# Gated cross-attention and ternary feed-forward block: two weight pieces scaled on GpSimd, one load and three steps of the start reordered

## What is computed

```python
x = x + tanh(g_xattn) * (softmax(q k^T / 8) v @ Wo + bo)      # q from layernorm(x), k and v from the context, 8 heads
g = bitlinear(layernorm(x), w_gate)                            # bitlinear: activations rounded to 8 bits per row,
u = bitlinear(layernorm(x), w_up)                              # weights to -1, 0, 1 by their mean magnitude
x = x + tanh(g_ffn) * bitlinear(square(relu(g)) * u, w_down)
```

## Time and profile before

| | before |
|---|---|
| time, median of 3 runs | 1199.75 us (1198.95 to 1201.97) |
| the profiled execution | 1198.77 us, span 1197.0 us |
| TensorE busy | 1177.8 us (98%) |
| DVE busy | 1032.1 us (86%) |
| ScalarE busy | 868.9 us (73%) |
| GpSimd busy | 306.5 us (26%) |
| longest chain | PE 88%, DVE 5%, DMA 3%, ACT 2% |

### The profile page before, as it was taken

The page is one execution under the profiler, slowest core; times in us unless marked ns, Lnnn a source line. Parts: engine busy times, 40 slices in busy tenths (PEclk is TensorE's granted clock), DMA queues, the critical chain, the costliest instruction groups (busy, mean ns, idle before and its releaser), DMA issues.

```text
span 1197.0 us, 18708 instructions
## 1 busy us (share of the span) xinstructions
PE 1177.8 (98%) x5859; PEld 743.8 (62%) x5859; DVE 1032.1 (86%) x2123; ACT 868.9 (73%) x928; POOL 306.5 (26%) x313
## 2 busy tenths in 40 slices
PE   8998999999999999999999999999999999999997
PEld 7655566656665666666566656665666666566653
DVE  4888898888989888888998888889898888888876
ACT  4877767777886777677877767776787677767763
POOL 3231222222442222222442222222244222222200
PEclk9999999999999999999999999999999999999999
DMA  9695535444444464344444464444444444344422
GB/s 353 251 294 125 148 96 102 114 101 99 96 114 98 112 176 110 95 104 106 101 99 101 114 182 102 97 113 98 107 97 106 96 98 114 101 99 100 98 65 57
DMA packets 286269, 144.61 MB, mean 121 GB/s; under 512 B 254509, under 2 KB 254893, under 8 KB 283684
## 3 DMA queue, kind: packets, MB, share of 16 engines
q1 hardware_dynamic: 286240, 144.32, 47.3%
q10 hardware_dynamic: 4, 0.00, 0.0%
HBM read 57.86 MB, written 24.35 MB: 69 GB/s over the span
## 4 chain that ended last, share of the span: by engine, by line
PE 88%; DVE 5%; DMA 3%; ACT 2%; issue 2%; SPq 0%; POOL 0%; DVEq 0%; ACTq 0%
PE gu_ps L1020 35%; PE o_ps L988 18%; PE s_ps L66 17%; PE y_ps L1034 17%; DMA v_scr<-x 1%; DMA xf_sb<-in_x_feat 1%; DVE half_max L1269 1%; PE gu_ps L1147 1%; DMA x_sb<-in_x_tok 0%; DVE staged L1376 0%; DVE staged L1263 0%; ACT staged L754 0%; ACT staged L797 0%; PE gu_ps L1119 0%; ACT staged L760 0%
## 5 line engine op out<-in xcount | busy, mean ns | idle before, releaser
L1020 PE MATMUL gu_ps<-w_gate,xq_t 128*128 128x512 bf16 x1016 | 240.9, 380 | 7.6 <-DVE staged L1263 7.6
L1020 PE MATMUL gu_ps<-w_up,xq_t 128*128 128x512 bf16 x1024 | 241.9, 379 | 0.0
L1034 PE MATMUL y_ps<-w_down,hq_t 128*128 128x512 bf16 x1008 | 228.0, 379 | 1.4 <-DMA hq_t<-staged 1.3
L988 PE MATMUL o_ps<-v_sb,pt_high 128*128 128x512 f32 (+1 forms) x640 | 212.9, 413 | 0.7 <-DVE pt_low L1252 0.7
L1263 DVE TENSOR_TENSOR staged<-staged,gu_ps 128x1024 f32<-128x1024 f32 x128 | 155.6, 1215 | 61.4 <-ACT staged L760 61.4
L66 PE MATMUL s_ps<-a_sb,xf_high 128*128 128x308 f32 x1024 | 187.3, 305 | 0.0
L1020 PEld LDWEIGHTS gu_ps<-w_up,xq_t 128*128 128x128 bf16 x1024 | 100.3, 98 | 120.8 <-ACT staged L754 0.3
L620 POOL TENSOR_TENSOR rstd<-var_eps,neg_half 128x1 f32<-128x1 f32 x128 | 95.7, 747 | 307.6 <-DVE var_eps L1228 269.5
L1034 PEld LDWEIGHTS y_ps<-w_down,hq_t 128*128 128x128 bf16 x1008 | 98.6, 98 | 120.7 <-DMA hq_t<-staged 1.8
L797 ACT ACTIVATE staged<-staged,h_scale 128x1024 f32<-128x1024 f32 x126 | 137.9, 1141 | 46.1 <-DVE h_scale L1283 46.1
L1020 PEld LDWEIGHTS gu_ps<-w_gate,xq_t 128*128 128x128 bf16 x1016 | 94.3, 98 | 120.1 <-issue 5.6
(11 more groups left out here) (142 smaller groups left out, 1439.3 us busy)
## 6 DMA issues: line engine op xcount, KB each, us to landing
xf_sb<-in_x_feat SPq DMA_DIRECT2D x64, 256.0 KB, 2.6
x_sb<-in_x_tok SPq DMA_DIRECT2D x64, 256.0 KB, 2.8
y<-staged SPq DMA_DIRECT2D x64, 256.0 KB, 2.1
staged<-in_wg_t SPq DMA_DIRECT2D x4, 1024.0 KB, 10.5
staged<-in_wd_t SPq DMA_DIRECT2D x4, 1024.0 KB, 7.2
folded<-a_scr SPq DMA_DIRECT2D x3, 1232.0 KB, 5.8
v_scr<-x SPq DMA_DIRECT2D x12, 256.0 KB, 2.8
folded<-v_scr SPq DMA_DIRECT2D x3, 1024.0 KB, 4.9
```

What stands on the lines that cost most here:

```text
L988: last = nc.tensor.matmul(o_ps[:, :], pt[0:rows, P * c:P * (c + 1)], v_sb[0:rows, v, c, :], start=(c == 0 and pt is pt_high and v == 0), s ...
L1020: last = nc.tensor.matmul(target[:, q, :], xq_t[:, s.par(0), c, :], w[:, c, cols], start=(c == 0), stop=(c == DC - 1))
L1034: last = nc.tensor.matmul(y_ps[:, :], hq_t[:, c, :], w_down[:, c, :], start=(c == 0), stop=(c == FC - 1))
```

## The change

- SP loads the value weights ahead of the query weights.
- `scale(2, 2)` and `scale(2, 3)` go from ScalarE's step 0 to GpSimd, behind `normalise(start, 2)` and ahead of its step 0, as one tensor_scalar each (multiply, add; 128 x 2048, float32).
- In step 1 ScalarE does `relu_half(1, 0)` and `square_half(1, 0)` first, ahead of `part_probs(3)` and `mark_hidden(0)`.
- On DVE `probs_low` of tile 1 goes from the head of step 0 to between `ternary(2, 0)` and `ternary(2, 1)`.

```diff
@@ SP, start
                 sp.dma_start(wkv_sb[:, 0, 2, :], wk[:, 2, :]).then_inc(wk_loaded[2], 16)
+                sp.dma_start(wkv_sb[:, 1, :, :], wv).then_inc(wv_loaded, 16)
                 sp.dma_start(wq_sb, wq_t).then_inc(q_loaded, 16)
-                sp.dma_start(wkv_sb[:, 1, :, :], wv).then_inc(wv_loaded, 16)
@@ GpSimd
+                def scale(m, p):
+
+                    pool.wait_ge(unit_inv_done, m + 1)
+                    pool.wait_ge(weight_stage[m][p], MEASURED)
+                    nc.gpsimd.tensor_scalar(scaled_slot(m, p), raw(m, p), inv_unit[:, m:m + 1], ROUND,
+                                            ALU.mult, ALU.add).then_inc(weight_stage[m][p], 1)
+
...
                 normalise(start, 2)
+                scale(2, 2)
+                scale(2, 3)
                 steps_by_batch(pool, step, (2, 3, 4, 5), split_keys, split_values)
@@ ScalarE, step
                 def step(s, split=None, b=None):
+                    if s.opens(1):
+                        relu_half(s, 0)
+                        square_half(s, 0)
                     if s.has(2):
                         part_probs(s, 2)
...
-                    if s.has(0):
+                    if s.has(0) and not s.opens(1):
                         relu_half(s, 0)
                         square_half(s, 0)
-                    if s.opens(0):
-                        scale(2, 2)
-                        scale(2, 3)
@@ VectorE, step and start
-                    if s.has(1) and not s.opens(1):
+                    if s.has(1) and not s.opens(0) and not s.opens(1):
                         probs_low(s, 1)
...
                 ternary(2, 0, w_down)
+                probs_low(start, 1)
                 ternary(2, 1, w_down)
```

## The result

The changed kernel takes 1202.4 us (median of 20 runs) against 1199.98 for the kernel before (20 runs). The ratio is 1.0023, 95% interval 1.0017 to 1.0029: 2.8 us slower, with 2.0 to 3.5 as the interval. One of its runs took 1335 us at a granted clock of 0.85 and is not part of the ratio. The forecast was +2.8 us. The loss is under the 0.3% (3.6 us) that the prediction named as what can be told from no change, but its interval leaves out 0.

A forecast was written before the change was run, and what follows sets the result against it. The prediction took DVE as the path from 84.78 us on, with TensorE's gaps its shadow. Its terms 0 - 0.3 + 0.8 - 1.0 + 3.3 = +2.8 us on 1199.75 gave 1202.6 us, range 1198.0 to 1206.5.

The forecast's parts named there:

- Part 1: Start, value weights loaded first: project_values gap goes, fold_keys(1, 0) still starts at 25.73; 0 us, bounds -1.7 and +0.5.
- Part 2: DVE, pt_low of tile 1 ahead of ternary(2, 1): TensorE's 0.75 us gap goes; -0.3 us, bounds -0.4 and 0.
- Part 3: ScalarE without two scales: GpSimd's low_part(4) comes earlier and meets DVE's centred; +0.8 us, bounds 0 and +1.0.
- Part 4: ScalarE step 1, relu and square first: hidden_half(1, 0) earlier, mark_input(2) then limits; -1.0 us, bounds -1.4 and 0.
- Part 5: Two scales on GpSimd, 1.9 us each: DVE waits for them and runs late; +3.3 us, bounds 0 and +9.7.
- my deduction of 0.26: DVE beside GpSimd's scales: each delays DVE by its 1.9 us length less 0.26, 3.3 us for two.
- A: Rival: GpSimd's scale is slow, over 2.3 us each, taking the sum past +3.6 us; chance 0.27.
- B: Rival: DVE keeps the ports, hiding the first scale; +1.2 us, 1200.9 us; chance 0.09.
- C: Rival: DVE-GpSimd exclusion costs nothing here; -0.5 us, 1199.2, or 1198.4 without the low_part(4) collision; chance 0.08.
- D: Rival: faster, the load order's 1.78 us comes through; -3.0 us, 1196.7, if exclusion also costs nothing; chance 0.06.

The follow-up runs named there:

- e1: Kernel before with only the value weights loaded ahead of the query weights; ratio 0.9998 (0.9989 to 1.0007).
- e4: Kernel before with only pt_low of tile 1 moved between the two ternary pieces on DVE; ratio 0.9992 (0.9984 to 1.0001).
- e2: Kernel before with only the two down-piece scales moved from ScalarE to GpSimd; ratio 1.0044 (1.0031 to 1.0058).
- e11: Kernel before, scales left on ScalarE, plus two GpSimd operations of the same shape on other data that nobody waits for; ratio 1.0047 (1.0033 to 1.0060).
- e5: Changed kernel with the old load order; ratio 1.0016 (1.0007 to 1.0025) against the kernel before.
- e3: Kernel before with only relu and square first in ScalarE's step 1; ratio 0.9988 (0.9977 to 0.9998).
- e7: Changed kernel with GpSimd scaling only 1024 of 2048 columns of each piece, the rest left unscaled; ratio 0.9999 (0.9990 to 1.0008) against the kernel before.
- e9: Kernel before with relu first, pt_low early, value weights first and four filler products on TensorE behind fold_keys(0, 3); 1196.9 us, ratio 0.9977.

## Why the prediction was right

The sign and the main mechanism (DVE waits for GpSimd's two scales) were right. That the size agrees so closely (+2.8 forecast, +2.8 measured) is luck: a term of 0.8 us that is not there stands in the sum, and the measured time holds a lower clock that the sum has no term for. Part by part:

- **Part 1, load order (0 us).** Not contradicted: e1's -0.2 (-1.3 to +0.8). The mechanism shows in the traces: `fold_keys(1, 0)` starts at 24.4 to 25.9 in the seven traces with the new order, and at 25.0 to 25.7 in the five with the old order whose clock stayed up. What the forecast had no term for is a lower clock behind the larger gap. In the changed kernel the 32 products from `fold_keys(1, 0)` on took 6.11 us in place of 4.54.
- **Part 2, pt_low (-0.3, bounds -0.4 and 0).** The stretch of e4 showed -0.52, outside my bounds by 0.1.
- **Part 3, collision of low_part(4) with centred (+0.8, bounds 0 and 1.0).** The step that failed: in the changed kernel it is 0. The mechanism exists, 0.74 us in e2 and e11 and 0.28 in e5, but whether the two instructions meet turns on tenths of a microsecond. In the changed kernel DVE and GpSimd have moved against each other: `low_part(4)` starts at 100.05 beside a ternary instruction, and this time GpSimd waits (1.85 us instead of 1.27) while DVE's `centred` keeps 0.49 us. I placed the collision by times of before, although part 5 moves DVE by 3.3 us. Against `scale(2, 1)`, `centred` came 3.15 us later than before and `low_part(4)` 0.4 earlier. GpSimd's and DVE's timelines of the changed kernel:

```profile
100.05 1.85 POOL L601 TENSOR_TENSOR xf_low<-xf_sb,xf_high 128x512 fp32r<-128x512 f32 x1 [1.68 <-ACT xf_high L678]
```

```profile
100.05 0.69 DVE L1416 TENSOR_SCALAR w_down<-w_down 128x2048 bf16<-128x2048 bf16 x1
...
102.39 0.49 DVE L1311 TENSOR_SCALAR centred<-x,mean_var 128x512 f32<-128x512 f32 x1
```

- **Part 4, relu first (-1.0, bounds -1.4 and 0).** -0.86 in e3, with both named followers (the wait for the transposed planes, the neighbour `low_part(5)`) in the rows, and -1.52 in the changed kernel's own trace, outside the bounds, where the planes landed 3.8 us after their issue and not 4.4.
- **Part 5, GpSimd's scales (+3.3).** Two waits of 1.66 us, 3.3 in all. The operation lasts about 1.8 us for 2048 columns against my 1.9, and my deduction of 0.26 was about 0.1 too large; the two cancel.

The sum of what e2 to e4 show is 3.3 - 0.9 - 0.5 = +1.9, not +2.8. In the changed kernel's own trace the stretch grew by 1.14: +2.66 up to the second `hidden_half` (parts 5 and 2) and -1.52 behind it (part 4). The trace's 2.64 us are this 1.14 and 1.50 ahead of it. Of the 1.50, the lower clock between 26 and 30 us is 1.57; the earlier start of `fold_keys(1, 0)` takes back 0.47, and longer waits of TensorE up to 82 us add 0.4. So the total came out right with 0.8 us of part 3 in it that isn't there. By the timed runs +1.9 (e5) and +2.8 (changed) can't be told apart; whether the load order makes the rest stays open.

Two smaller readings of the prediction were off as well. Not all of TensorE's idle time lies before 130 us: 11.5 us do, but 1.9 more lie between 130 and 1180 us and the rest at the very end. And the gap of 1.82 us ahead of `gate_up(1, 0)` was left out of those that the change can touch, though it grew by 1.20. Neither moves the sum, which was made on DVE's path.

Of the rivals, A (slow GpSimd) falls with the 1.8 us, B (DVE keeps the ports) and C (no exclusion) with 4.13 and 2.88 us for DVE's instructions, and D (faster) with the ratio.

The changed kernel's gaps show the general point too: `gate_up(1, 0)` took 3.35 us for its eight products instead of 1.89, 1.5 us more on TensorE, and that cost nothing, because TensorE was not what anyone waited for: the gap ahead of `gate_up(2, 0)` was still 0.98 us. The same fall behind `gate_up(2, 0)` costs its full length (the 1072.9 us and more in seven traces).

## What to carry to other kernels

Before moving work to GpSimd, look at what VectorE does in those microseconds: beside scales and ternary pieces of 2048 columns, GpSimd's operation was added to VectorE's path almost in full (1.66 of about 1.8 us), even when nobody waited for its result (e11). Relieving an engine that isn't the path (ScalarE by 3.9 us here) brought nothing. And place collisions of moved work by the new times, after the largest shift has been applied.

## What the runs showed of the hardware

- GpSimd's tensor_scalar with two operations on float32 takes about 1.8 us for 128 x 2048, and its half 0.86 less: 0.84 ns a column, near the 0.87 of its plain write. The Trainium skill ("GPSIMD Engine Reference", Engine selection) has one-input operations at roughly line rate; the trace agrees.
- A GpSimd operation that waits goes in at the next boundary between two DVE instructions even when DVE's next one has no wait of its own: it went between the two scales, which stand back to back (the second took 2.92 us). It can also be GpSimd that waits: `low_part(4)` took 1.85 us instead of 1.27 beside a ternary instruction of the changed kernel.
- The granted clock of TensorE fell to about 0.5 (1.2 GHz instead of 2.4) for some 4 us (some 7 us once, in e11) after single idle gaps of 1.95 to 4.1 us, in some executions and not in others: after 3.02 us in the changed kernel and in e7, not after 3.02 us in e9; after 2.20 us in e5, not after 2.20 us in the changed kernel; after 2.23 us in e1 and e4, not after 2.23 us in e2. A window of the changed kernel behind the gap of 3.02 (0.62 from 110 to 112 us):

```profile
108.00:110.00 2.00, 1.50 (x4) 0.58 (x5) 2.00 (x3) 0.00 (x0) 0.00 (x0) 0.52 0.91 291
```

  One such fall adds about 1.5 us or more to TensorE's own time (3.35 us in place of 1.89 for eight products). That makes single profiled executions of this kernel differ by more than the effects looked for, and it is why the stretch was measured from a point inside the same trace; falls lie inside it too (changed, e2, e4, e5, e7, e11), and those of e2 and e11 delay DVE.
